# A macaron block on one core: low halves of transposed rows taken from SBUF, attention steps joined, and one FFN run moved ahead

## The reference

```
x = x + 0.5 * ffn(layernorm(x))
x = x + attn(layernorm(x))
x = x + 0.5 * ffn(layernorm(x))      # the same weights as the first
```

```
C = f*C + i * v k^T        n = f*n + i*k
h = C q / max(|n.q|, 1)
```

## Time and profile before

| | us |
|---|---|
| median of 3 runs | 939.15 (937.07 to 939.82) |
| the profiled execution | 939.06 |
| its span, first to last instruction | 936.9 |
| TensorE busy | 865.0 (92%) |
| VectorE, ScalarE, GpSimd busy | 627.0, 359.0, 244.5 |

### The profile page before, as it was taken

How to read it: one execution, slowest core, us unless ns; L and a number is a source line. 1 busy time by engine, 2 the same in 40 slices (tenths; PEclk the granted TensorE clock), 3 DMA queues, 4 the chain that set the end, 5 groups by cost and what they waited for, 6 DMA issues and landing times. The chain is left out here.

```text
span 936.9 us, 30800 instructions
## 1 busy us (share of the span) xinstructions
PE 865.0 (92%) x12744; PEld 823.7 (88%) x12744; DVE 627.0 (67%) x1502; ACT 359.0 (38%) x716; POOL 244.5 (26%) x234
## 2 busy tenths in 40 slices
PE   2958889999899998999899999999989989898998
PEld 2947869999799998999899998999979979898998
DVE  5445677585866858486676758677576787687642
ACT  4453152433533344243523436234343452233431
POOL 2013332320422313322322313332042234411110
PEclk9988999999999999999999999999999999999999
DMA  9105434212243202442133312431035035500000
GB/s 263 57 14 140 131 95 126 66 40 70 83 132 86 58 19 55 124 126 58 36 94 116 87 40 73 139 112 35 24 103 154 11 110 140 152 25 2 1 24 23
DMA packets 66313, 76.04 MB, mean 81 GB/s; under 512 B 12702, under 2 KB 48670, under 8 KB 66176
## 3 DMA queue, kind: packets, MB, share of 16 engines
q1 hardware_dynamic: 66176, 74.09, 28.2%
HBM read 56.75 MB, written 17.30 MB: 79 GB/s over the span
## 5 line engine op out<-in xcount | busy, mean ns | idle before, releaser
L644 ACT ACTIVATE r_h<-bank 128x512 fp32r<-128x512 f32 x128 | 76.5, 598 | 233.6 <-PE bank L1128 164.9
L1093 PE MATMUL bank<-xT_hi,wi_hi 128*128 128x256 f32 x512 | 148.1, 289 | 2.6 <-DVE r_l L836 1.8
L1093 PE MATMUL bank<-wo_hi,r_h 128*128 128x256 f32 x512 | 147.7, 288 | 1.1 <-DVE r_l L836 0.5
L1095 PE MATMUL bank<-xT_lo,wi_hi 128*128 128x256 f32 x512 | 144.1, 282 | 0.0
L1094 PE MATMUL bank<-xT_hi,wi_lo 128*128 128x256 f32 x512 | 144.1, 281 | 0.0
L1095 PE MATMUL bank<-wo_lo,r_h 128*128 128x256 f32 x512 | 143.7, 281 | 0.0
L1094 PE MATMUL bank<-wo_hi,r_l 128*128 128x256 f32 x512 | 143.7, 281 | 0.0
L836 DVE SCALAR_TENSOR_TENSOR r_l<-bank,r_h 128x512 fp32r<-128x512 f32 x128 | 87.9, 687 | 82.7 <-ACT r_h L644 82.1
L1093 PE MATMUL bank<-xT_hi,wgu_hi 128*128 128x256 f32 x352 | 103.1, 293 | 0.6 <-DVE gm L845 0.5
L1093 PEld LDWEIGHTS bank<-xT_hi,wi_hi 128*128 128x128 f32 x512 | 97.3, 190 | 5.0 <-DVE r_l L836 2.4
L1093 PEld LDWEIGHTS bank<-wo_hi,r_h 128*128 128x128 f32 x512 | 96.4, 188 | 3.9 <-issue 2.5
(11 more groups left out here) (157 smaller groups left out, 2143.9 us busy)
## 6 DMA issues: line engine op xcount, KB each, us to landing
dm<-f_scratch SPq DMA_DIRECT2D x128, 128.0 KB, 3.0
arena<-parts_scratch SPq DMA_DIRECT2D x96, 128.0 KB
arena<-parts_scratch SPq DMA_DIRECT2D x96, 64.0 KB
arena<-parts_scratch SPq DMA_DIRECT2D x32, 192.0 KB
x<-in_x SPq DMA_DIRECT2D x16, 256.0 KB, 3.0
parts_scratch<-pa SPq DMA_DIRECT2D x64, 64.0 KB
parts_scratch<-pb SPq DMA_DIRECT2D x64, 64.0 KB
parts_scratch<-pc SPq DMA_DIRECT2D x64, 64.0 KB
```

The lines of the kernel that those rows point to most:

```text
L644: nc.scalar.activation(flat(r_h[:, n]), U[use % 2][:], ACT.Relu).then_inc(f_rh, 1)
L1093: nc.tensor.matmul(dst, lh, rh, start=first, stop=False, **more)
L1095: return nc.tensor.matmul(dst, lh, rl, start=False, stop=last, **more)
```

## The change

1. RUNS begins with 1(0), 1(1), A(0), 1(2), A(1): the first FFN of block 1 comes ahead of the projections of block 0.
2. In FFN runs VectorE makes xT_lo from x32 in SBUF and no longer from the bank. The transposes of the second half and the routing wait for ScalarE's copy (g_x32), no longer for the remainder (g_lo). ScalarE's next xn now waits for the remainders of the FFN run before.
3. The very first run's second half is transposed into bank S0 (`turned`).
4. Both units' scores of a chunk are one step. A step of M forms the state of chunk j+1, then both units' values and the carry of chunk j. The state moves from bank W to the free end of bank M. On VectorE the folding of the state is a stream of its own (C).
5. All five strings of ORDER are redrawn for that.

```diff
-RUNS = [("1", 0), ("A", 0), ("1", 1), ("A", 1), ("1", 2)]
+RUNS = [("1", 0), ("1", 1), ("A", 0), ("1", 2), ("A", 1)]
...
-        3G U G 5U V 2U V 2U 2V 4U V U V U 2V 2G 5U G U G 2U G U G 7U V 2U V 2U 2V 4U S U V S Y V 2U M 2V M 2S M 2Y M G 2S Y G 3U M 2U M U M Y S U S G 2Y M U G
+        3G 2U G 5U V U 2V U G U V 2U G U G 2U 2V U G 2V 5U V 2U V U 2V U G 3U V U G V 3U 2V 6U 2G U G 2U G 5U G 2U V M U S U 2V 2U V G 2U S M 3U V Y V 2U V Y
...
+        def turned(r, h):
+
+            return S0 if r.i == 0 and h == 1 else G
...
                         act.wait_ge(g_gate, r.k)
+                        if r.i and RUN[r.i - 1].ffn:
+                            act.wait_ge(g_lo, 2 * r.i)
...
-                        nc.scalar.copy(xT_h[:, r.i % 2, h].rearrange("p c t -> p (c t)"), G[:]).then_inc(g_hi, 1)
+                        nc.scalar.copy(xT_h[:, r.i % 2, h].rearrange("p c t -> p (c t)"), turned(r, h)[:]).then_inc(g_hi, 1)
                         yield
                         if r.ffn:
-                            nc.scalar.copy(x32[:, h].rearrange("p c t -> p (c t)"), G[:]).then_inc(g_x32, 1)
+                            nc.scalar.copy(x32[:, h].rearrange("p c t -> p (c t)"), turned(r, h)[:]).then_inc(g_x32, 1)
...
                         if r.ffn:
+
                             dve.wait_ge(g_x32, 2 * r.k + h + 1)
-                        v.tensor_tensor(to, G[:], hi, ALU.subtract).then_inc(g_lo, 1)
+                            v.tensor_tensor(to, x32[:, h].rearrange("p c t -> p (c t)"), hi, ALU.subtract).then_inc(g_lo, 1)
+                        else:
+                            v.tensor_tensor(to, G[:], hi, ALU.subtract).then_inc(g_lo, 1)
...
-            def Y_():
+            def C_():
+
+                added = M[:, H * HV:H * HV + DC * 4 * HV].rearrange("p (c e m d) -> p c e m d", c=DC, e=2, m=2)
                 for b, j in chunks:
                     n = b * TILES + j
-
-                    added = W[:, 0:DC * 4 * HV].rearrange("p (c e m d) -> p c e m d", c=DC, e=2, m=2)
...
                     dve.wait_ge(a_state, n + 1)
+                    if j:
+
+                        dve.wait_ge(a_c, n)
                     dve.wait_ge(a_ex[1], n)
...
+                        elif r.ffn:
+                            if r.i:
+                                pe.wait_ge(g_x32, 2 * r.k + 1)
                         else:
                             pe.wait_ge(g_lo, 2 * r.i + 1)
...
                     if r.ffn:
-                        pe.wait_ge(g_lo, 2 * (r.i + 1))
+                        pe.wait_ge(g_x32, 2 * (r.k + 1))
...
             def M_():
-                for b in range(BLOCKS):
-                    for u in range(UNITS):
...
+                def state(b, j):
+
+                    pe.wait_ge(a_wv, NG * (TILES * b + j + 1))
+                    for c in range(DC):
+                        for q in range(COLS):
+                            tile = slice(q * P // COLS, (q + 1) * P // COLS)
+                            of = c * P + q * P // COLS
+                            done = nc.tensor.matmul(M[tile, H * HV + c * 4 * HV:H * HV + (c + 1) * 4 * HV], k32[:, b % 2, j, of:of + P // COLS],
+                                                    wv[:, HH * c + 2 * q:HH * c + 2 * q + 2].rearrange("p h m d -> p (h m d)"),
+                                                    start=True, stop=True)
+                    done.then_inc(a_state, 1)
+
+                heads = M[:, 0:H * HV].rearrange("p (h m d) -> p h m d", m=2, d=HV)
+                for b, j in chunks:
+                    n = TILES * b + j
+                    if j == 0:
+
+                        if n:
+                            pe.wait_ge(a_y, n)
+                            pe.wait_ge(a_at[1], DC * n)
+                            pe.wait_ge(a_at[0], DC * n_on(*chunks[n - 1]))
+                        state(b, j)
+                        yield
+
+                    pe.wait_ge(a_at[1], DC * (n + 1))
+                    pe.wait_ge(a_at[0], DC * n_on(b, j))
+                    if n:
+                        pe.wait_ge(a_y, n)
+                    if j < TILES - 1:
+                        state(b, j + 1)
+                    pe.wait_ge(f_read, a_use(b, A_V + j // 2) + 1)
+
+                    for g in range(NG):
+                        u = NG * n + g
+                        pe.wait_ge(a_P, u + 1)
...
                         done.then_inc(a_O, 1)
...
+                    pe.wait_ge(a_ex[1], n + 1)
+                    pe.wait_ge(a_qc, DC * (b + 1))
+                    if not opens(b, j):
+                        pe.wait_ge(a_ex[0], n_on(*chunks[n - 1]))
...
                     done.then_inc(a_c, 1)
+                    yield
```

More of the change, by code:

```diff
@@ L1250, in G_ @@
                             for jj in range(2):
-                                done = nc.tensor.transpose(G[:, (c * 2 + jj) * P:(c * 2 + jj + 1) * P],
+                                done = nc.tensor.transpose(turned(r, h)[:, (c * 2 + jj) * P:(c * 2 + jj + 1) * P],
                                                            xn[:, 2 * h + jj, c * P:(c + 1) * P], ident[:])
@@ L1314, in M_ @@
                         done.then_inc(a_O, 1)
[L1315 to L1333 removed]
+                    pe.wait_ge(a_ex[1], n + 1)
+                    pe.wait_ge(a_qc, DC * (b + 1))
+                    if not opens(b, j):
+                        pe.wait_ge(a_ex[0], n_on(*chunks[n - 1]))
+                    for m in range(1 if opens(b, j) else 0, 2):
+                        for c in range(DC):
+                            for q in range(COLS):
+                                tile = slice(q * P // COLS, (q + 1) * P // COLS)
+                                t = j * P + m * TH + q % 2 * (P // COLS)
+                                of = c_ex[m][:, c].rearrange("p (h e d) -> p h e d", e=2, d=HV)[:, :, q // 2]
+                                done = nc.tensor.matmul(heads[tile, HH // 2 * c:HH // 2 * (c + 1), m], q32[:, b % 2, c, t:t + P // COLS], of,
+                                                        start=False, stop=True, skip_group_check=True)
+                    done.then_inc(a_c, 1)
+                    yield
             def Y_():
@@ L1339, in Y_ @@
                         pe.wait_ge(a_zz, n)
-                    pe.wait_ge(a_wv, NG * (n + 1))
-                    for c in range(DC):
-                        for q in range(COLS):
-                            tile = slice(q * P // COLS, (q + 1) * P // COLS)
-                            of = c * P + q * P // COLS
-                            done = nc.tensor.matmul(W[tile, c * 4 * HV:(c + 1) * 4 * HV], k32[:, b % 2, j, of:of + P // COLS],
-                                                    wv[:, HH * c + 2 * q:HH * c + 2 * q + 2].rearrange("p h m d -> p (h m d)"),
-                                                    start=True, stop=True)
-                    done.then_inc(a_state, 1)
-                    yield
-                    pe.wait_ge(a_at[1], DC * (n + 1))
-                    pe.wait_ge(a_at[0], DC * n_on(b, j))
                     pe.wait_ge(a_y, n + 1)
```

111 lines of the change are left out of this document (43 added, 68 removed).

## The result

The change made the kernel slower: 947.17 us median (944.59 to 950.56, 4 runs) against 938.11 of the kernel before beside it, ratio 1.0123, interval 1.0085 to 1.0161 (the ratio is estimated from the single runs; the quotient of the two medians is 1.0097). A second set of six runs on another chip gave 1.0109, 1.0059 to 1.0160. The profiled execution took 946.81 us with a span of 944.6. The forecast was 916.

What follows compares the result with a forecast made beforehand. TensorE, busy 92% of the span, sets the time and only its lost time can be won. Terms -7.5 - 5 + 1 - 3 - 7.4 - 2.3 = -24, taken as -23: 939 to 916 us, range 901 to 934.

Steps and rivals of the forecast that it cites:

- 1 hole: Before block 0's projections: block 1's first FFN fills TensorE's idle gap; -7.5 us (bounds 0 and -8.0).
- 2 projections of block 0: Block 0's projections: the 4.2 us remainder wait goes and TensorE comes in warm; -5 us (bounds 0 and -9).
- 3 start: Kernel start: correction product slightly earlier, first down product later, near 31.5; together +1 us (bounds -3 and +4).
- 4 remainder: FFN runs: transposes and routing wait for ScalarE's copy alone, not VectorE's remainder; -3 us (bounds 0 and -4).
- 5 joint steps: Attention: fewer visits of narrow matmuls, 0.21 us saved each; -7.4 and -2.3 us (bounds together -5 and -11).
- 6 attention of block 0: Block 0's attention: thinner cover from FFN(2) and block 1's projections costs no more than before; 0 (bounds -5 and +8).
- 7 ring of dm: Joint attention steps waiting on three dm buffers: loop about 7.3 us fits available work; 0, at most +36 us.
- 8 other waits: Other waits of a block's 4 us idle time: redrawn, not removed; 0 (bounds -6 and +6).
- rival B: Hole only moved: block 0's attention loses its filler and pays part back; 928 us, chance 0.18.
- C: More goes: the idle 4 us per block halves over seven blocks; 905 us, chance 0.16.
- D: Slower side: late dm loads stall most joint steps with a next state by 1.5 us; 952 us, chance 0.10.
- E: VectorE's remainder with two SBUF inputs is stretched beside GpSimd, 26 us; 941 us, no change, chance 0.06.

Runs made afterwards that it cites:

- the part alone: Kernel before, old order, with only the remainder taken from the SBUF copy and the first run's second half transposed into a spare bank: 937.56 us, ratio 1.0035.
- Putting y first: Changed kernel with seven y copies moved earlier in VectorE's order, ahead of routing or remainder steps: 955.29 us, 1.0218 of the kernel before.
- start mended: Changed kernel with the start of TensorE's, VectorE's and ScalarE's queues rewritten: 942.38 us, 1.0086 of the kernel before.
- edges moved: Changed kernel with rewritten start, plus 76 or 248 instructions of small products ahead of TensorE's work: 943.66 us (1.0077) and 944.92 us (1.0107).
- the seam mended: Changed kernel's rewritten start up to the first gate/up product, old order behind, GpSimd following the changed order past those steps: 940.54 us, 1.0033 of before.

## Why the prediction was wrong

The place of each difference, in the profiled executions:

| step | forecast | seen |
|---|---|---|
| 1 hole | -7.5 | -8, gone |
| 2 projections of block 0 | -5 | +1 |
| 3 start | +1 | about +5 |
| 4 remainder | -3 | waits gone, others in their place; the part alone 1.0035 |
| 5 joint steps | -9.7 | about -6.5, busy time at equal clock |
| 6 attention of block 0 | 0 | about +6 |
| 7 ring of dm | 0 | 0 |
| 8 other waits | 0 | +9.7, all idle time gained from L(0) on, with step 4 in it |

Ahead of L(0): -8 + 1 + 5 + 6, and about -2 of step 5, give +2, and 177.5 - 175.2 is 2.3. From L(0) on: +9.7 of idle time, about -5 of step 5 and half a microsecond of clock give +5.4, which is what that part grew.

*Step 1 was right*, and so was *step 5* in its mechanism: changes between wide and narrow matmuls fell from 228 to 136, which are the 114 and 68 visits of the prediction. Its size was taken too large. The row of 64 matmuls in 0.58 us ended in a narrow product and so had no exit in it. To the next wide product a score step of 64 takes 0.63 us in the changed kernel, one of 32 0.35 before, medians over the ten visits of each kind without idle time at the upper level, so a pair joined saves 0.15 and not 0.21:

```profile
186.69 0.70 PE L1307 MATMUL bank<-arena 96*32 96x64 bf16 x64
187.33 0.39 PE L1108 MATMUL bank<-xT_hi,wgu_hi 128*128 128x256 f32 x1
```

*Step 8 failed, and it weighs most.* The prediction put it as "The other waits of a block's 4 us are redrawn, not removed: 0, bounds -6 and +6". Idle time in the block of L(0) went from 4.0 to 7.35 us, in the tail from 26.7 to 33.1: 9.7 together, outside the bound. Two things fill it. In the block it is waits for copies of y on VectorE, 4.6 us where there was none. In the tail it is mostly the issue stops, 11.0 us where 5.3 stood; waits for y (5.6, 1.6 before) and u_rep (2.6, none) came, those for the remainder (3.7) and z (2.3) went and others shrank, which nearly cancels. The copies of y are late where VectorE's queue takes selection steps first. One of these took 1.11 us instead of 0.19, once in 16, beside GpSimd's product of 248.83 to 249.98:

```profile
248.69 0.19 DVE L999 TENSOR_TENSOR won<-lg,lmax 128x32 f32<-128x32 f32 x1
248.92 1.11 DVE L1001 TENSOR_TENSOR won<-won,prio 128x32 f32<-128x32 f32 x1
...
252.03 0.42 DVE L1085 TENSOR_TENSOR y<-bank,den 128x256 f32<-128x256 f32 x1
```

Putting y first does not win it back. What I got wrong is the kind of thing that this idle time is. I treated it as a list of waits, from which step 4 takes its own off and which a shorter TensorE stream leaves alone. In the runs it belongs to the order as a whole: 26.3 to 28.6 us in the tail behind several heads and with or without the remainder from SBUF in the old order, 32.9 to 34.4 in the new one, start mended or not, edges moved or not. Waits came in place of those that went, with y moved, with the seam mended, and with the remainder in the old order. A reason that fits is slack between chains on five queues: when TensorE saves 0.15 us per visit, it arrives earlier at results that are no earlier. But the larger part of the rise in the tail is issue stops, which are no waits for results as far as the profile shows, and why the new order has twice as many microseconds of them was not found.

*Step 3* was mis-sized by about 4 us. The first down product came 6.5 us later than before; as in the prediction, one more up product (1.4) was done ahead of it, which leaves +5. Its chain (weights, then lora_b) was the right one, but it left out that ScalarE's table load of 1.28 us moves with the first activation behind the first wait, and it had lora_b ready from 21.8 + 2.4, where its conversions ran from 24.49 to 26.96, behind a subtraction that waited for ScalarE. It took bounds of -3 and +4, too narrow for a queue redrawn on three engines. The mended start confirms the cause: 21.27.

*Step 2* expected the wait on the remainder to go and nothing to follow. The projections of block 0 idle 8.6 of 25.9 us at a granted clock of 0.74; before it was 7.6 of 25 at 0.82. The wait on the remainder (4.2) went and waits of 3.3 (ScalarE's copy) and 2.7 (VectorE's gm) came, while "TensorE comes in warm" was worth nothing: the clock was at the lower level from 94.4 to 108.1, where an idle time of 3.35 us had just ended at 92.9 and one of 2.73 lies within.

*Step 6* failed in size. From 108.2 to L(0) TensorE idles 13.2 us at 0.90, before from 110 to L(0) 7.3 at 0.95, and about as many matmuls lie in both (1023, 1030). It took 69.3 us, 65.2 before, in spite of some 2 us that the joint steps save. With block 1's FFN moved ahead there is less wide work to lay into these gaps; that this is the cause is argued from the order, and no run tested it alone. It is rival B's mechanism, at about +6 instead of its +4, and with step 2 wholly lost.

The clock is a term that the prediction had only inside its steps 2 and 6. Ahead of L(0) TensorE was busy at the lower level for 25.0 us, 16.6 before, about 4 us of cost by the same estimate as above, which are part of the steps 2, 3 and 6.

*The rivals.* B is right as far as it goes, and explains 11 of the 31 us between forecast and result. C did not happen. D falls: no wait of TensorE for the weighted values (wv) or the scan over 0.5 us in the changed kernel. E falls by the row of L983. None of the rivals was that the redrawn queues lose, from L(0) on, more than the joint steps win; a chance of 0.10 for slower was far too small for a change that rewrites five queues by hand.

The sign by which the prediction said it would be wrong came true: the first gate/up product was not before 170, and the block after it grew; the later ones did not all grow (from the second to the third gate/up run 110.6 us in both kernels).

## What to carry to other kernels

When an engine is 92% busy and its idle time is spread over many short waits with different releasers, a saving on it need not be worth its length: here 6.1 us less busy time in the tail stood against 6.3 us more idle time, and mending one wait after another moved it. Before busy times of two profiles are compared, look at the granted clock of each stretch: 2 of those 6.1 us were clock, and so were 2 us that looked like the gain of the remainder. Cost a redrawn order at the same size as the edits it carries, with a bound on the slower side at least as wide as all savings together. Filler moved into one hole is missing at the place it came from, in wide work and in clock, so cost both ends.

## What the runs showed of the hardware

- TensorE stops for up to 3.6 us at some of the places that lie 256 instructions apart, mostly in long bursts of narrow matmuls; the places follow the count of instructions, not the code: 76 instructions ahead of the work move them, 248 leave seven of eight in their steps.
- ScalarE's table load (1.28 us) stands directly ahead of its first activation. Where that is the conversion of weights, the load ran at 0.74 and the activation itself waited for its DMA until 7.43; where it is the normalised rows, with semaphore instructions ahead of it, the load ran behind them, at 8.03.
- Wide products start 0.21 us apart at the lower level of the clock and 0.12 at the upper one. Ahead of the 13.7 us at the lower level from 94.4 on TensorE had idled 3.35 us.
- A selection step of 128x32 on VectorE with two inputs in SBUF took 1.11 us instead of 0.19, once in 16, while GpSimd ran a 128x512 product, but the remainder of 128x512 from SBUF stayed at 682 ns in the median of 32.
